# Attention with routed experts: where the second half of a unit's values and sums is issued

## The reference

```python
xn = layernorm(x)                                  # x: 32 x 256 x 128
q  = (xn @ Wq.T).reshape(b, t, 8, 32)
kv = xn @ Wkv_down.T                               # rank 64
k  = (kv @ Wk_up.T).reshape(b, t, 8, 32)
v  = (kv @ Wv_up.T).reshape(b, t, 8, 32)
attn = softmax(einsum('bqhd,bkhd->bhqk', q, k) * 32**-0.5)
a  = einsum('bhqk,bkhd->bqhd', attn, v).reshape(b, t, 256) @ Wo.T
idx = mod(floor(xn @ wr + br), 8)                  # one expert for each token
y  = relu(xn @ W1[idx] + b1[idx]) @ W2[idx] + b2[idx]
out = x + a + y
```

## Time and profile before

| | |
|---|---|
| median of 3 runs | 508.06 us (507.12 to 509.37) |
| the profiled execution, its own time | 513.86 us |
| its span, first to last instruction | 512.0 us |
| PE busy | 459.1 us, 90% |
| DVE busy | 418.5 us, 82% |
| POOL busy | 378.0 us, 74% |
| ACT busy | 346.2 us, 68% |
| mean granted clock of PE | 0.966 |

### The profile page before, as it was taken

How to read it: one execution, slowest core, us unless ns; L and a number is a source line. 1 busy time by engine, 2 the same in 40 slices (tenths; PEclk the granted TensorE clock), 3 DMA queues, 4 the chain that set the end, 5 groups by cost and what they waited for, 6 DMA issues and landing times.

```text
span 512.0 us, 15093 instructions
## 1 busy us (share of the span) xinstructions
PE 459.1 (90%) x4992; PEld 320.8 (63%) x4992; DVE 418.5 (82%) x898; ACT 346.2 (68%) x864; POOL 378.0 (74%) x387
## 2 busy tenths in 40 slices
PE   1766769899999999997999999997999999999977
PEld 1355435456566465666999999984666656657635
DVE  6878997677998888975788888885698898898865
ACT  3677446666777777775777777765687587677664
POOL 4544266888888888854777777776698888988962
PEclk9985798999999999999999999999899999999999
DMA  8675213444747588599787898844365556756422
GB/s 241 222 168 128 61 52 86 120 103 94 201 118 192 150 235 251 156 261 235 218 270 236 269 276 265 252 132 99 88 138 140 134 127 139 144 108 146 97 73 63
DMA packets 81930, 83.07 MB, mean 162 GB/s; under 512 B 10608, under 2 KB 66384, under 8 KB 81872
## 3 DMA queue, kind: packets, MB, share of 16 engines
q1 hardware_dynamic: 77520, 73.40, 52.8%
q0 software_dynamic: 4352, 8.92, 7.1%
HBM read 38.61 MB, written 18.37 MB: 111 GB/s over the span
## 4 chain that ended last, share of the span: by engine, by line
PE 62%; DVE 15%; DMA 6%; issue 6%; SPq 5%; ACT 4%; POOL 2%; DVEq 0%; ACTq 0%; POOLq 0%
PE psum L1269 9%; PE psum L1234 8%; PE psum L1253 7%; DVE negm L975 6%; PE psum L1392 5%; PE psum L1311 4%; PE psum L1284 4%; PE psum L1375 3%; PE psum L1393 3%; PE psum L1376 3%; PE psum L1377 3%; SPq L324 3%; PE psum L1182 3%; DMA stk<-mT 2%; PE psum L1183 2%
## 5 line engine op out<-in xcount | busy, mean ns | idle before, releaser
L686 ACT ACTIVATE prob<-psum 128x512 f32<-128x512 f32 x256 | 150.1, 593 | 103.9 <-PE psum L1253 82.2
L975 DVE TENSOR_REDUCE negm<-psum 128x2 f16<-128x512 f32 x256 | 170.8, 682 | 46.1 <-PE psum L1234 40.1
L603 POOL TENSOR_TENSOR padd<-prob 128x512 f32<-128x512 f32 x104 | 126.7, 1218 | 36.2 <-ACT prob L686 27.3
L1234 PE MATMUL psum<-stk 96*128 96x256 f16 x512 | 102.4, 282 | 11.6 <-DVE negm L975 10.8
L554 POOL TENSOR_TENSOR padd<-xTl,padd 128x512 f16<-128x512 f32 x71 | 82.2, 1158 | 34.8 <-DVE padd L1087 34.8
L1253 PE MATMUL psum<-stk 97*128 97x256 f16 x512 | 99.1, 277 | 6.8 <-DMA stk<-mT 3.5
L756 ACT ACTIVATE xTl<-psum,xn_all 128x128 f32<-128x128 f32 x284 | 80.9, 368 | 27.6 <-POOL padd L554 17.1
L572 POOL DMA_INDIRECT xsort<-xn_all,pos x64 | 67.2, 1049 | 15.9 <-issue 13.8
L580 POOL DMA_INDIRECT xn_all<-ysort,pos x64 | 65.7, 1026 | 14.0 <-issue 7.5
L1234 PEld LDWEIGHTS psum<-stk 96*128 96x128 f16 x512 | 42.1, 99 | 53.9 <-DVE negm L975 27.1
L1269 PE MATMUL psum<-prob,vt 128*32 128x256 f32 x1024 | 70.5, 394 | 0.6 <-ACT prob L686 0.6
(11 more groups left out here) (167 smaller groups left out, 889.9 us busy)
## 6 DMA issues: line engine op xcount, KB each, us to landing
stk<-split SPq DMA_DIRECT2D x192, 128.0 KB
xn_all<-wsplit SPq DMA_DIRECT2D x71, 258.0 KB, 4.6
xTh<-xsort SPq DMA_DIRECT2D x18, 256.0 KB, 4.3
ysort<-xTh SPq DMA_DIRECT2D x18, 256.0 KB, 4.6
out<-acc SPq DMA_DIRECT2D x15, 256.0 KB
acc<-x SPq DMA_DIRECT2D x3, 1024.0 KB, 8.0
xn_all<-W SPq DMA_DIRECT2D x12, 256.0 KB
wsplit<-xn_all SPq DMA_DIRECT2D x12, 256.0 KB
```

What stands on the lines that cost most here:

```text
L603: nc.gpsimd.tensor_tensor(padd[:, bb, hs], prob[:, bb, hs, 0, :], prob[:, bb, hs, 1, :], ALU.add).then_inc(pool_add, 1)
L686: nc.scalar.activation(prob[:, bb, h, :, :].rearrange("p a c -> p (a c)"), bank[st_bank(u, n)], ACT.Exp, scale=SCALE).then_inc(act_exp, 1)
L975: V.tensor_reduce(negm[:, k % 2, col:col + 2], bank[n % 2].rearrange("p (a c) -> p a c", a=2), AX.X, ALU.max, negate=True).then_inc(dve_ma ...
L1234: ins = mm(bank[n % 2][:, qc * T:(qc + 1) * T], stk[0:96, s, 1, h, t0 + qc * P:t0 + (qc + 1) * P], stk[0:96, s, 0, h, t0:t0 + T], start=Tr ...
```

## The change

PE issues values and sums of both halves of a unit in one block at the end of step 7. The step 2 block goes, and with it the two calls that stood behind the loops (ahead of `hidden(0)` and of `last_proj`). The wait for `dve_rank`, which guards a PSUM bank in unit 0, moves with it. On DVE the last `key_add` of unit u moves from step 0 of unit u + 1 to step 7 of unit u, behind that step's `row_max` and ahead of `residual`.

```diff
-                        if n == 0 and not f and not (last and k == 3):
-                            key_add(u - 1, 7, 2 - half)
...
+                        if n == 7 and not (last and k >= 2):
+                            key_add(u, 7, 2 - half)
                         if n == 7 and k % 2 == 1 and not (first and half == 0 and k == 1):
                             residual(it * 2 + k // 2 - 1)
...
-            key_add(NU // 2 - 1, 7, 2)
...
-                        if n == 2 and half == 0 and first and k == 1:
-                            pe.wait_ge(dve_rank, 2)
-                        if n == 2 and not f:
-                            values(u * 2 - 1, k + 3, 1, it * 2 + (k + 1) // 2 * 2)
-                            sums(u - 1, 1, last and k == 3, half)
...
                         if n == 7:
                             values(u * 2, k, 0, sbu * 2 + 1, u + 2 if nxt else u + 1)
                             sums(u, 0, last and k >= 2, half)
+                            if f and half == 0:
+                                pe.wait_ge(dve_rank, 2)
+                            values(u * 2 + 1, k, 1, sbu * 2 + 2)
+                            sums(u, 1, last and k >= 2, half)
...
-            values(NU - 1, 3, 1, NU // 2)
-            sums(NU // 2 - 1, 1, False, 0)
...
-            values(2 * NU - 1, 3, 1, NU)
-            sums(NU - 1, 1, True, 1)
```

## The result

The changed kernel takes 554.88 us (median of 4 runs, 552.79 to 555.23) against 507.59 for the kernel before in the same session: 1.0905 times as long, 95% interval 1.0871 to 1.0939, or +47.3 us. The forecast was 545.5, so it had the sign, and it was 9.4 us short. The time lies in the stated range of 529 to 559, but 0.9 us above the 535 to 554 that the prediction gave as the forecast's own range. The profiled execution took 552.79 us, span 550.9.

A forecast was written before the change was run, and what follows sets the result against it. PE sets the pace with POOL the second engine without slack; waits close rings through POOL and ACT. 3.5 + 10 - 2.8 + 2.5 + 22 + 2.3 = +37.5 on median 508.0 gives 545.5 us; own range 535 to 554, stated range 529 to 559.

The forecast's parts named there:

- The ring through POOL: Units 16 to 29: sums wait for POOL's last add, whose successor needs PE's later work; turns 11.9 us for 10.06, +22.
- DVE as near rival: Second half: DVE's key_add ends within 0.1 us of POOL's last add; some 3 us more if last every turn.
- The ring through ACT, units 3 to 14: ACT's exp chain plus the second half's 1.43 us: 10.4 us per plain unit, 11.4 with weight split; +10 (+5 to +12).
- The first units: Units 0 to 2: the moved wait for DVE's second rank sum delays proj_q of unit 1; +3.5 us (2 to 5).
- Before the experts: Unit 15's second half fills PE's 2.14 us idle, and unit 14's longer period shortens the transfer wait; -2.8 (-3 to -1).
- Unit 16 to 17: First add of unit 17 comes 1.3 us later, and half clock after PE's stand costs about 1.2; +2.5 (1.3 to 3).
- The end: From unit 29 on: its turn and the delayed scores_T of unit 31, less the missing step 2 block; +2.3 (0 to 4).
- The median: Final step: the +37.5 us worked out from one profile was added to the median 508.0, giving 545.5; profiled execution 551.4.
- clock rival: Second half: PE's stands bring 1.2 GHz in each second turn, +12, time 558; chance 0.12.
- The ring not binding: Units 17 to 29: POOL's last add arrives before PE reaches the sums, +5 instead of +22, time 529; chance 0.13.
- Faster: PE is the bound, so one block saves small gaps in 28 units and the seam's 2.8; about 502; chance 0.03.
- no change: Whole kernel: later turns make up what the rings cost, so no change shows; chance 0.02.

The follow-up runs named there:

- h2_only: Against the kernel before, the change made in units 16 to 31 only, units 0 to 15 keeping the old order: 539.38 us, ratio 1.0595.
- two_heads_es: Changed kernel with POOL's step 6 add in units 16 to 29 given to DVE's key_add, and expert_sum moved behind key_add: 536.35 us, ratio 1.0539.
- two_heads: Changed kernel, units 16 to 29: POOL leaves out the add of step 6 and DVE's key_add does both heads: 546.01 us, ratio 1.0728.
- gather_late: Changed kernel with POOL's third gather, in units 16 to 31, behind the add of step 6 instead of ahead: 546.76 us, ratio 1.0759.
- low_behind: Changed kernel with DVE's expert weight split (units 7, 9 to 13) and table of experts (units 6, 8) moved behind key_add: 548.80 us, ratio 1.0791.
- unit0_back: Changed kernel with only unit 0's second half, and its wait for the second rank sum, back in step 2 of unit 1: 551.56 us, ratio 1.0826.
- seam_only: Kernel before with only unit 15's second-half values and sums issued ahead of the experts' first transposition: 508.14 us, ratio 1.0004.
- before_again: The kernel before, unchanged, profiled a second time: one execution, 507.25 us, span 505.4, where the first profile had span 512.0.
- mT_late: Changed kernel with PE's transposition of the maxima moved from step 3 to step 4, and ACT's copy behind exp 4: 552.51 us, ratio 1.0869.

## Why the prediction was right in kind and short in size

**What bounds.** Right. The reading of POOL as the second engine without slack was the step that carried the forecast: h2_only and two_heads_es show that the adders set the second half: POOL ends last, and DVE ends 0.58 us ahead of it.

**The ring through POOL.** Forecast 3.58 + 8.28 + 0.05 = 11.9, measured 3.61 + 8.47 + 0.05 = 12.13. For twelve turns that is +23.6 against the first profile and +22.5 against the second, where +22 was expected. Two small errors partly offset each other: eleven turns are 0.2 longer, because key_add now starts ahead of POOL's last add and that add takes 0.94 instead of 0.73, and the last turn is 1.0 shorter than forecast, because unit 29 has no proj_q and proj_k. The wait in even units is 1.58, not 1.2; 0.2 of that is the longer add. The step "POOL has no gap in it now and gets none, so it neither shrinks nor grows" was wrong by that 0.2.

**DVE as near rival.** Placed within 0.1 us of POOL's add; in unit 22 it ended 0.58 us ahead of it (444.43 against 445.01). It did not end the turns, as forecast. Where POOL is out of the way, in two_heads and gather_late, it does.

**The ring through ACT, units 3 to 14.** Forecast +10, measured +13.1 against the second profile and +14.5 against the first, from which it was worked out; +14.5 lies above the term's own range of +5 to +12. This is the term that was mis-sized most. The plain even unit is 10.43 against 10.4, to the hundredths what 5.83 + 3.15 + 1.43 gave. The units with a split are 11.0 in even ones against 11.4: the split makes ACT's stretch from exp 0 to the end of exp 5 6.51 us (168.50 to 174.43 + 0.58 in unit 9), 0.7 more and not 0.95. What failed is the estimate of 2.2 for the odd units. Plain ones take 11.2, and those with a split 12.2 to 12.4, 0.8 to 1.4 above even ones of their kind, where 2.2 in all, some 0.4 in each of six, was allowed; and units 6 and 8 took 11.94 and 11.37 although I had counted them as plain. low_behind gives 6.4 us of it back: DVE's work on expert data in step 6 stands ahead of a key_add that is now waited for. The prediction did name "DVE's weight split" among what delays key_add, but put a lump of some tenths on it, where in the other half it had followed DVE's queue to the end of key_add; the table of experts in units 6 and 8 it didn't name. The 0.8 that is left in odd units after low_behind (10.42 and 11.2) I put down to the output projection, 16 matmuls, 1.95 us in all, that PE does there between exp 1 and step 7; it was not taken out in a run.

**The first units.** Forecast +3.5, measured +2.5 against the first profile and +4.8 against the second, the fastest start of four. The wait was where it was said to be: PE's values start at 69.47, where the second rank sum was to end at 69.4. unit0_back gives 3.3 us by the medians, 1.1 by the first add of unit 3.

**Before the experts.** Forecast -2.8, measured -1.5 against the first profile and +0.2 against the second, and seam_only shows no clear gain when it is done by itself. The term had two halves. The 1.43 us of work did go into the idle time. The 1.4 that unit 14's longer period was to give did not come: in the changed kernel PE waits 0.70 us more behind the 1.43 that now stand ahead, 2.13 together, where it had waited 2.14.

```profile
248.31 0.41 PE L1363 MATMUL psum<-ident,xTh 128*128 128x128 f32 x2 [0.70 <-DMA xTh<-xsort]
```

The 2.14 was one profile's; a second has 1.55 there, and filling it brought 0.6 us back as a wait for DVE's xTl. How much of the 1.43 a typical run keeps stays open.

**Unit 16 to 17.** The move itself was forecast as +1.3 on the distance in the first profile, 11.7, and measured 11.61. The 1.2 added for half clock did not come in this profile: PE stood 2.26 us and the stretch around it kept a granted clock of 1.00.

```profile
370.00:376.00 6.00, 3.74 (x33) 2.08 (x30) 2.66 (x4) 1.69 (x4) 3.22 (x5) 1.00 0.12 28
```

It did come in others. Four more kernels have the same order and the same stand there: h2_only (2.24 us, clock 1.00, distance 11.60), mT_late (2.24), low_behind (2.23) and unit0_back (2.25). In the last three the clock was half for 3.4 us right behind it, and the distance was 12.79, 12.91 and 12.02. PE in low_behind, its timeline and its table by stretches:

```profile
364.18 0.91 PE L1284 MATMUL psum<-padd,ones 128*32 128x256 f32 x8 [2.23 <-POOL padd L603]
...
364.00:368.00 4.00, 3.82 (x20) 1.86 (x21) 0.89 (x2) 0.62 (x2) 1.09 (x2) 0.57 0.13 33
```

So the +1.2 fits two of the three and is too much for the third, and it is the price of something that happens in some executions and not in others.

**The end.** +2.3 forecast, +3.0 measured against the second profile; against the first it would be -1.5, so the base decides here.

**The median.** The step that failed in the method is "taking the same difference on the median". The profiled execution of before was 5.8 us above the median, most of it from a stall at its end, and 551.4 was forecast for the profiled execution of after, which took 552.79. By that profile the change costs 38.9, close to the 37.5, but in part by luck: the 4.5 too little for units 3 to 14 and 1.6 for the second half's ring are hidden by a tail that came out 3.8 lower, because the first profile's stall is in its base. Against before_again, which lacks the stall, the sum was short by 8.0 us (45.5 against 37.5): 3 from the seam, 3 from the units with odd numbers or expert work, 1.3 from the start, 0.7 from the tail and 0.5 from the ring, less 0.7 at unit 16. The remaining 1.8 of the 47.3 is mostly that after's profiled execution was its shortest. And the time is in the stated range by luck as well: the range's upper part, 554 to 559, was there for the clock rival, which is not what made the kernel slower.

**The rivals.** The clock rival fell: a stand of about 1.6 to 1.9 us in each even turn, and 1.00 from 380 to 510 us. It is not ruled out for every execution, since unit0_back has half clock from 518 us on, behind the last such stand (1.89 us). The ring not binding fell (529): h2_only alone is at 539. Faster and no change fell with the sign.

## What to carry to other kernels

Before you move a consumer in an in-order queue, ask of each producer it waits for whether that producer's next input stands behind the consumer: if so the wait closes a ring, and the ring's length, added up row by row, is the new period (11.9 forecast, 12.13 measured). Then look at what is queued ahead of each producer in its own queue, in every kind of unit, since the first delay that you find (POOL's, 8 to 9 us) hides a second (DVE's expert_sum, 9 to 10 us), and another kind of unit has its own (late_low, 6 us). An idle time in one profile isn't a gain until you know what is late next. A profile that lies 1% above its median should be compared with a second one before a difference is carried over to the median.

## What the runs showed of the hardware

DVE and POOL stretch each other's instructions by more than I had thought, in both directions: expert_sum takes 0.68 us with no add of POOL beside it, 1.81 in the earlier trace rows and 2.20 in the changed kernel; key_add of one head 0.42 and 0.70 to 0.76; POOL's single add 0.73 and 0.94. Where POOL's single add starts 0.26 us ahead of key_add, only key_add gets longer; where key_add starts 0.34 us ahead, both do. TensorE's granted clock did not follow the length of single stands in a plain way: after 3.10 us (at 69.47) and after 2.26 us (at 372.44) the stretch stayed at 1.00, and after 2.57 us (at 77.53), eight microseconds behind the first, the stretch from 77 to 82 us had 0.66. Columns as in the earlier trace rows:

```profile
66.00:74.00 8.00, 4.59 (x50) 2.35 (x42) 5.75 (x15) 1.90 (x5) 1.80 (x3) 1.00 0.01 2
...
77.00:82.00 5.00, 4.47 (x29) 3.10 (x33) 4.88 (x10) 2.85 (x7) 4.36 (x4) 0.66 0.53 147
```

In before_again a stand of only 1.80 us, ahead of unit 17's scores at 353.94, stands before a stretch at 0.72, though PE had been busy only 2.20 of the 4 us before it:

```profile
350.00:354.00 4.00, 2.20 (x30) 0.90 (x23) 1.28 (x3) 0.75 (x2) 3.75 (x4) 1.00 0.54 83
354.00:360.00 6.00, 6.00 (x48) 3.27 (x49) 3.12 (x6) 3.85 (x9) 3.40 (x4) 0.72 0.47 123
```

The clearest case is the stand ahead of unit 16's sums: 2.23 to 2.26 us in five profiles, half clock behind it in three of them and not in the other two. So the length of one stand doesn't decide; what does, these runs don't tell.
